# Who adds the state's part to the skip term: GpSimd instead of VectorE, in a state-space stage on one Trainium2 core

## The chip, the core and the metric

The kernel runs on one core of one Trainium2 chip. Its engines have queues of their own: TensorE (PE in the profile, its weight loads PEld), VectorE (DVE), ScalarE (ACT), GpSimd (POOL) and SyncE (SP, which here only starts transfers). They wait for each other through semaphores alone. The metric is device time in microseconds, median of the runs; lower is better.

## The reference, cut to what matters

The program is a stack of four layers on 1024 tokens of width 512 (2 sequences of 512): a state-space layer, a gated feed-forward layer, an attention layer and a mixture of experts, each followed by a layer norm and a residual. The change lies in the first. Its core, for each of 64 heads of 64 channels, is

```
state = state * dA_t[..., None, None] + dtx_t[..., None] * B_t[:, :, None, :]
y_t = jnp.einsum('bhpn,bhn->bhp', state, C_t)
...
y = jnp.moveaxis(ys, 0, 1) + x * D[None, None, :, None]
```

after which y is normalised over groups of 512 channels, multiplied by silu(gate), and projected back to width 512.

## The kernel before, in words

The state-space layer goes over 8 groups of 8 heads (512 channels). The first and the last group are written out, the six between are one hardware loop, so all engines repeat one pattern with a period of about 126 us. A group has 8 steps, s = 0 to 7, one for each block of 128 tokens; a sequence has 4 blocks, and c = (s - 1) % 4 is the place in its sequence of the block that is finished in step s. Work is pipelined over steps: step s prepares block s (transposes, decay masks), computes y of block s - 1, and projects the normalised yn of block s - 2. In steps 0, 1, 2, 4, 5 and 6 two convolution tiles of the next sequence or group go between (their taps on VectorE, their tanh on ScalarE); the last group has them only in steps 0 to 2.

For one block, y has three parts:

- the state's part, C times the carried state: TensorE writes it into bank 6 (L1352), VectorE scales it with the decays into `y` (L1060, signals `yo_used`); only where c > 0
- the part of the block's own 128 tokens, 16 matmuls on the diagonal block into bank 7 (L1358, signals `yi_ready`)
- the skip term `xd` = x * D, made by GpSimd one step earlier (L597, signals `xd_ready`)

VectorE adds the second (L1073, `y_part`) and then the third (L1076, `y_ready`). Where c = 0 there is no state's part, and one addition (L1080) does it. After `y`, in VectorE's order: the new state (L1089, which needs GpSimd's decayed state, L578), the first convolution tile's silu (L972), the taps of the second (L966, three), the gate (L1099), the second silu, the output's accumulation (L1106), and at the head of the next step `yn` (L1033), for which TensorE's transposes L1344 wait.

GpSimd's order in a step is: the two decay masks `am` of the next block (L551, these need `d_ready`, the end of TensorE's L1325), in step 2 the four low halves of the output weights (L299, `wol`), the state's decay (L578, c = 1 and 2), `dtx` (L588, needs the 16 matmuls done), `xdec` (L593), `xd` (L597, needs `y_ready`), and the two small operations of the normalisation (L602, L605). In step 3 two low halves of the next group's convolution weights follow (`wcl`, L299). TensorE's L1325 waits for the taps of all convolution tiles issued before it, since it writes a bank that they read.

The order of each engine is what is written in its `step` function; nothing schedules it anew.

Of the kernel before, what the change touches and what calls it, by code (L numbers as in the profile page):

```python
# [18 lines left out]
NT = NB * L // P  # L19
# [34 lines left out]
def program(nc, hidden, w_conv, w_gate, w_dt, conv_w, conv_b, dt_bias, A_log, Dskip, norm_w, w_out,  # L54
            ff_gu, ff_dn, gate_s, up_s, down_s, wq, wk, bqk, wv, bv, wo, bo, gate_w, expert_w, out):
    ctx = ExitStack()
    with ctx:
# [4 lines left out]
        def sem(name):  # L62
            return ctx.enter_context(nc.semaphore(name))
# [4 lines left out]
        def bk(i):  # L68
            return banks[:, i, :]
# [23 lines left out]
        def sa(name, shape, dt=F32):  # L93
            return sb(name, shape, dt, A)
# [26 lines left out]
        xd = sa("xd", [P, GI])  # L121
        bcast = xd[:, 0:2 * H].rearrange("p (a h) -> p a h", a=2)
        state = sa("state", [P, GI])
        y = sa("y", [P, GI])
# [111 lines left out]
        am_ready, xd_ready, xdec_ready, dtx_ready, sdec_ready = (sem(s) for s in ("am_ready", "xd_ready", "xdec_ready", "dtx_ready", "sdec_ready"))  # L236
        m_ready, yo_ready, yo_used, yi_ready, y_part, y_ready = (sem(s) for s in ("m_ready", "yo_ready", "yo_used", "yi_ready", "y_part", "y_ready"))
# [42 lines left out]
        def conv_stage(group):  # L280

            t = xbc[:, :, :].rearrange("p a b -> p (a b)") if group == 0 else x[:, :, :].rearrange("p a b -> p (a b)")
            return t[:, 0:KT * CT * P].rearrange("p (k c) -> p k c", k=KT)
# [3 lines left out]
        def pair(ap):  # L287
            return ap.rearrange("p (h c) -> p h c", h=HG)
# [8 lines left out]
        def low(eng, o, full, high):  # L297

            return eng.tensor_tensor(o, full, high.bitcast(F32), ALU.subtract)  # L299
# [23 lines left out]
        def entered(g, i):  # L323

            return (CH - 1) * NB * g + (CH - 1) * (i // CH)
# [42 lines left out]
        def heads(row):  # L368

            return cur[:, row, :].unsqueeze(2).to_broadcast([P, HG, HP])  # L370
# [162 lines left out]
        def _(pool):  # L533
# [14 lines left out]
            def decays(i):  # L548

                for part, a in enumerate((ah, al)):  # L550
                    m = pool.tensor_tensor(am[:, part, :, :], a[:, i, :].bitcast(F32).unsqueeze(2).to_broadcast([P, HG, P]),  # L551
                                           upto[:, :].unsqueeze(1).to_broadcast([P, HG, P]), ALU.mult)
                m.then_inc(am_ready, 1)
# [8 lines left out]
            def step(g, s, first, last):  # L562
                if s < NT and not (last and s == NT - 1):

                    pool.wait_ge(d_ready, NT * g + s + 1)
                    if s == NT - 1:
                        pool.wait_ge(ah_ready, g + 2)
                    decays((s + 1) % NT)
                if s == 2:
                    for k in range(KT):  # L570
                        pool.wait_ge(wo_hi, KT * g + k + 1)
                        low(pool, wol[:, k, :], out_stage[:, k, :], woh[:, k, :]).then_inc(wo_lo, 1)
                i = s - 1
                c = i % CH
                if s >= 1 and 1 <= c < CH - 1:

                    pool.wait_ge(yo_ready, entered(g, i) + c)
                    pool.tensor_tensor(pair(state[:, :]), pair(state[:, :]), heads(4 * NT + i),  # L578
                                       ALU.mult).then_inc(sdec_ready, 1)
                if s == 0:  # L580
                    pool.wait_ge(cur_ready, g + 1)
                if s < NT:

                    pool.wait_ge(x_out, NT * g + s + 1)
                    src = pair(xtok[:, s % 2, :])
                    if not (first and s == 0):
                        pool.wait_ge(yi_ready, NT * g + s)
                    pool.tensor_tensor(pair(dtx[:, :]), src, heads(NT + s), ALU.mult).then_inc(dtx_ready, 1)  # L588
                    if s % CH < CH - 1:
                        m = entered(g, s) + s % CH  # L590
                        if not (first and s == 0):
                            pool.wait_ge(st_ready, m)
                        pool.tensor_tensor(pair(xdec[:, :]), src, heads(3 * NT + s), ALU.mult).then_inc(xdec_ready, 1)  # L593
                if s < NT:
                    if not (first and s == 0):
                        pool.wait_ge(y_ready, NT * g + s)
                    pool.tensor_tensor(pair(xd[:, :]), src, heads(5 * NT), ALU.mult).then_inc(xd_ready, 1)  # L597
                if not (first and s == 0) and s <= NT:

                    n = NT * g + s  # L600
                    pool.wait_ge(ss_ready, n)
                    pool.tensor_tensor(ssv[:, i % 2:i % 2 + 1], ss[:, i % 2:i % 2 + 1], epsc[:, :],  # L602
                                       ALU.add).then_inc(ssv_ready, 1)
                    pool.wait_ge(ssv_ready, n)
                    pool.tensor_tensor(rg[:, i % 2:i % 2 + 1], ssv[:, i % 2:i % 2 + 1], mhalf[:, 0:1],  # L605
                                       ALU.pow).then_inc(rg_ready, 1)

                if s == 3 and not last:
                    for k in (2, 3):
                        pool.wait_ge(wc_hi, KT * g + KT + k + 1)  # L610
                        low(pool, wcl[:, k, :], conv_stage(1)[:, k, :], wch[:, k, :]).then_inc(wc_lo, 1)
                if s == NT - 1 and not last:
                    gate_low(g + 1)
                if last and s >= 3:
                    if s == 3:
                        pool.wait_ge(x_again, 16 * NT)
                    norm_pool(1, s - 3)

            def gate_low(g):
                for k in range(KT):  # L620
                    pool.wait_ge(wg_hi, KT * g + k + 1)
                    low(pool, wgl[:, k, :], gate_stage[:, k, :], wgh[:, k, :]).then_inc(wg_lo, 1)

            pool.wait_ge(ah_ready, 1)
            decays(0)
            gate_low(0)
            group_steps(pool, step)
            for n in range(NT - 1, ROUNDS):
                norm_pool(1, n)
            if STAGES >= 2:  # L630
                norm_wait(pool, 1, "tr", NT)
                pool.memset(acc[:, :, :], 0.0).then_inc(f_clear, 1)
                if STAGES >= 3:
                    c = Count(sel_ready)
# [22 lines left out]
                    for j, (base, step) in enumerate(((63, -1), (-64, 1))):  # L657
                        made(pool.affine_select(out=head[:, j:j + 1], in_=ones[:, 0:1], compare_op=ALU.is_ge, fill=0.0,
                                                base=base, pattern=[[0, 1]], channel_multiplier=step))
# [6 lines left out]
                for n in range(-2, ROUNDS):  # L666
                    if n >= 0:
                        norm_pool(2, n)
                    i = n + 2
# [278 lines left out]
        def _(dve):  # L948
# [70 lines left out]
            def step(g, s, first, last):  # L1019
# [7 lines left out]
                i = s - 2  # L1027
# [24 lines left out]
                i, c = s - 1, (s - 1) % CH  # L1052
                if not (first and s == 0) and s <= NT:
                    m = entered(g, i)
# [6 lines left out]
                i = s - 2  # L1061
# [5 lines left out]
                    low(nc.vector, ynTl[:, :], bk(4), ynTh[:, :]).then_inc(ynT_lo, 1)  # L1067
                i, c = s - 1, (s - 1) % CH
                if not (first and s == 0) and s <= NT:
                    if c > 0:  # L1070
                        dve.wait_ge(yi_ready, NT * g + i + 1)
                        dve.wait_ge(yo_used, m + c)
                        nc.vector.tensor_tensor(y[:, :], y[:, :], bk(7), ALU.add).then_inc(y_part, 1)  # L1073
                        dve.wait_ge(xd_ready, NT * g + i + 1)
                        dve.wait_ge(y_part, m + c)
                        nc.vector.tensor_tensor(y[:, :], y[:, :], xd[:, :], ALU.add).then_inc(y_ready, 1)  # L1076
                    else:
                        dve.wait_ge(yi_ready, NT * g + i + 1)
                        dve.wait_ge(xd_ready, NT * g + i + 1)
                        nc.vector.tensor_tensor(y[:, :], bk(7), xd[:, :], ALU.add).then_inc(y_ready, 1)  # L1080
                    if c < CH - 1:
                        dve.wait_ge(st_ready, m + c + 1)
                        if c == 0:
                            if not (first and s == 1):
                                dve.wait_ge(yo_ready, m)
                            nc.vector.tensor_copy(state[:, :], bk(6)).then_inc(state_ready, 1)
                        else:
                            dve.wait_ge(sdec_ready, (CH - 2) * NB * g + (CH - 2) * (i // CH) + c)
                            nc.vector.tensor_tensor(state[:, :], bk(6), state[:, :], ALU.add).then_inc(state_ready, 1)  # L1089
# [13 lines left out]
                i = s - 2  # L1103
                if not (first and s < 2):
                    dve.wait_ge(o_ready, NT * g + i + 1)
                    nc.vector.tensor_tensor(acc[:, i % NT, :], acc[:, i % NT, :], bk(1), ALU.add).then_inc(out_added, 1)  # L1106
                    if last and i >= 0:
                        norm_round(1, i)

            group_steps(dve, step)  # L1110
            norm_vector(1, NT)
            if STAGES >= 2:
# [45 lines left out]
            if STAGES >= 3:  # L1158
# [25 lines left out]
                for n in range(UNITS + O_BACK - 7):  # L1184
# [35 lines left out]
                    if piece:  # L1220
                        m, what, i, u = piece
# [444 lines left out]
```

## Time and profile before

| what | value |
|---|---|
| three runs | 1919.59 to 1921.9 us, median 1921.78 |
| the profiled execution | 1919.35 us, its span 1917.6 us |
| busy share of the span | PE 90%, DVE 69%, POOL 50%, ACT 38% |
| mean granted TensorE clock | 0.95 of full speed |
| the state-space groups in the span | about 88 to 1117 us |

The span runs from the first to the last instruction of the core; the execution's own time is 1.75 us longer. In the rows, a start and a duration are in us, the bracket at the end is the time that the engine stood idle before the instruction and who ended it, and an engine that is busy may still be blocked within an instruction: then its duration is longer than that of its fellows. One group serves as the pattern below: its step 2 is from 488.2 to 505.1 us.

### The profile page before, as it was taken

What the parts mean: (1) busy time and instruction counts of PE and PEld (TensorE: products, weight loads), DVE (VectorE), ACT (ScalarE), POOL (GpSimd) and SP (SyncE); (2) the same over time, 40 slices, a digit from 0 to 9 for tenths busy, and PEclk for the clock granted to TensorE, in tenths of its full rate; (3) what the DMA queues carried; (4) which work ended last, traced back from release to release, by engine and by line L of the source; (5) the groups of instructions that cost most, each with busy time, mean ns of one, the idle gap of its engine ahead of it and who ended that gap; (6) DMA issues with size and microseconds to landing.
All of it is one profiled execution on the core that took longest, in us unless ns stands there. A gap on an engine that the chain in (4) does not pass through costs nothing.

```text
span 1917.6 us, 25666 instructions
## 1 busy us (share of the span) xinstructions
PE 1725.5 (90%) x9030; PEld 1348.3 (70%) x9030; DVE 1316.7 (69%) x2025; ACT 728.0 (38%) x1338; POOL 966.5 (50%) x821
## 2 busy tenths in 40 slices
PE   3799999999999999999997769992899999878998
PEld 2578777777788777877786558881667776647886
DVE  4788787888777878788877555566267767663224
ACT  2443434434434344344352123330166766520010
POOL 3375676767757766677576441007333433151223
PEclk9899999999999999999998869995899999989999
DMA  3001020010100200101002002120000000101101
GB/s 128 1 34 45 1 77 1 33 44 0 53 24 0 77 0 33 44 0 77 0 1 77 1 28 75 68 77 33 0 12 1 12 1 1 46 4 63 44 22 44
DMA packets 16290, 61.31 MB, mean 32 GB/s; under 512 B 5472, under 2 KB 5600, under 8 KB 10976
## 3 DMA queue, kind: packets, MB, share of 16 engines
q1 hardware_dynamic: 16224, 60.44, 8.7%
q8 instruction: 40, 0.66, 0.1%
q14 instruction: 26, 0.21, 0.0%
HBM read 58.34 MB, written 2.10 MB: 32 GB/s over the span
## 4 chain that ended last, share of the span: by engine, by line
PE 70%; DVE 13%; POOL 8%; issue 5%; ACT 3%; SPq 0%; DMA 0%; POOLq 0%; DVEq 0%; ACTq 0%
PE banks L294 38%; PE banks L1426 6%; PE banks L1358 5%; PE banks L1545 3%; POOL wol L299 2%; PE banks L1436 2%; PE banks L1367 2%; PE banks L1504 2%; PE banks L1325 2%; PE banks L1352 2%; PE banks L1535 2%; DVE tap L966 2%; PE banks L1344 1%; DVE yn L1033 1%; DVE nmax L1189 1%
## 5 line engine op out<-in xcount | busy, mean ns | idle before, releaser
L966 DVE SCALAR_TENSOR_TENSOR tap<-banks,parg,tap 128x511 f32<-128x511 f32 (+2 forms) x288 | 214.8, 746 | 30.5 <-ACT tap L733 23.7
L551 POOL TENSOR_TENSOR am<-ah,upto 128x1024 fp32r<-128x1024 f32 x64 | 128.5, 2008 | 206.0 <-PE banks L1325 191.1
L688 POOL TENSOR_SCALAR kz<-kst,head 128x512 fp32r<-128x512 f32 x64 | 99.0, 1565 | 160.2 <-DVE kst L1173 160.2
L294 PE MATMUL banks<-xTh,wch 128*128 128x512 f32 x384 | 166.3, 433 | 3.1 <-POOL wcl L299 1.7
L1050 DVE TENSOR_TENSOR em<-em,gmask 128x1024 f32<-128x1024 f32 x64 | 130.9, 2046 | 49.1 <-ACT em L766 47.5
L551 POOL TENSOR_TENSOR am<-al,upto 128x1024 fp32r<-128x1024 f32 x64 | 160.3, 2505 | 0.0
L1358 PEld LDWEIGHTS banks<-dtx,em 128*128 128x128 f32 x1024 | 138.3, 211 | 28.8 <-issue 26.3
L294 PE MATMUL banks<-xTh,wcl 128*128 128x512 f32 x384 | 151.3, 394 | 0.0
L294 PE MATMUL banks<-xTl,wch 128*128 128x512 f32 x384 | 150.9, 393 | 0.0
L909 ACT ACTIVATE prob<-banks,nmax 128x128 f32<-128x128 f32 (+3 forms) x256 | 121.6, 529 | 55.1 <-DVE nmax L1189 54.9
L1358 PE MATMUL banks<-dtx,em 128*128 128x64 f32 x1024 | 134.9, 291 | 0.0
L1189 DVE TENSOR_REDUCE nmax<-banks 128x2 f32<-128x256 f32 (+3 forms) x128 | 104.7, 818 | 40.5 <-PE banks L1536 40.3
L1270 DVE SCALAR_TENSOR_TENSOR acc<-banks,we,acc 128x512 f32<-128x512 f32 x64 | 48.0, 751 | 121.1 <-PE banks L294 121.1
L733 ACT ACTIVATE tap<-banks,parg 128x512 f32<-128x512 f32 x96 | 74.6, 777 | 136.3 <-PE banks L294 128.7
L741 ACT ACTIVATE th<-tap 128x512 f32<-128x512 f32 x96 | 60.5, 631 | 152.4 <-DVE tap L966 149.6
L294 PE MATMUL banks<-wgh,xTh 128*128 128x512 f32 x256 | 111.9, 437 | 0.6 <-DVE tap L966 0.6
L294 PE MATMUL banks<-ewh,xTh 128*128 128x512 f32 x256 | 101.9, 398 | 5.2 <-DVEq L1266 5.2
L1545 PE MATMUL banks<-ident,prob 128*128 128x128 f32 x640 | 95.9, 277 | 10.6 <-DVE pB L1199 7.2
L294 PE MATMUL banks<-woh,ynTh 128*128 128x512 f32 x256 | 102.6, 401 | 1.5 <-DVE ynTl L299 1.5
L294 PE MATMUL banks<-wol,ynTh 128*128 128x512 f32 x256 | 102.4, 400 | 0.0
L294 PE MATMUL banks<-woh,ynTl 128*128 128x512 f32 x256 | 102.1, 399 | 0.0
L294 PE MATMUL banks<-wgl,xTh 128*128 128x512 f32 x256 | 101.3, 396 | 0.0
(244 smaller groups left out, 4622.2 us busy)
## 6 DMA issues: line engine op xcount, KB each, us to landing
x<-in_w_conv SPq DMA_DIRECT2D x7, 1536.0 KB, 6.6
x<-in_w_gate SPq DMA_DIRECT2D x8, 1024.0 KB, 4.8
x<-in_w_out SPq DMA_DIRECT2D x8, 1024.0 KB, 6.8
ew<-in_expert_w SPq DMA_DIRECT2D x8, 1024.0 KB, 4.8
gur<-in_ff_gu SPq DMA_DIRECT2D x7, 1024.0 KB, 4.9
x<-in_hidden SPq DMA_DIRECT2D x16, 256.0 KB, 4.0
dnr<-in_ff_dn SPq DMA_DIRECT2D x7, 512.0 KB, 3.4
out<-x SPq DMA_DIRECT2D x8, 256.0 KB, 2.0
```

The lines of the kernel that those rows point to most:

```text
L294: m = nc.tensor.matmul(o, a, b, start=first and n == 0, stop=last and n == len(terms) - 1)
L551: m = pool.tensor_tensor(am[:, part, :, :], a[:, i, :].bitcast(F32).unsqueeze(2).to_broadcast([P, HG, P]), upto[:, :].unsqueeze(1).to_broa ...
L688: m = pool.tensor_scalar(kz[:, quad % 2, p2, j, :], kst[:, p2, :].bitcast(F32), head[:, j:j + 1], None, ALU.mult)
L733: nc.scalar.activation(tap[:, q % 2, :], bk(CONV_BANKS[q % 2]), ACT.Identity, bias=parg[:, CT * KC + q:CT * KC + q + 1], scale=parg[:, KC ...
L741: nc.scalar.activation(th[:, :], tap[:, q % 2, :], ACT.Tanh).then_inc(tanh_ready, 1)
L909: e = nc.scalar.activation(prob[:, n % 2, j, 0:kw], bk(2 * (n % 2) + j)[:, 0:kw], ACT.Exp, bias=nmax[:, n % 2, j:j + 1])
L966: nc.vector.scalar_tensor_tensor(tap[:, q % 2, sh:L], bk(CONV_BANKS[q % 2])[:, 0:L - sh], parg[:, KC * q + k:KC * q + k + 1], tap[:, q % 2 ...
L1050: nc.vector.tensor_tensor(em[:, s % 2, :, :], em[:, s % 2, :, :], gmask[:, :].unsqueeze(1).to_broadcast([P, HG, P]), ALU.mult).then_inc(m_ ...
L1189: nc.vector.tensor_reduce(nmax[:, n % 2, :], banks[:, 2 * (n % 2):2 * (n % 2) + 2, 0:kw], AX, ALU.max, negate=True).then_inc(max_ready, 1)
L1358: m = mat(bk(7)[:, h * HP:(h + 1) * HP], em[:, i % 2, h, :], dtx[:, h * HP:(h + 1) * HP], start=True, stop=True)
L1426: m = mat(bk(2 * w + ft), gu[:, k, ft, w, :], part[:, k, tok], start=(k == 0 and part is xTh), stop=(k == KT - 1 and part is xTl))
L1545: m = pe.transpose(bk(4 + j)[:, c * P:(c + 1) * P], prob[:, w % 2, j, c * P:(c + 1) * P], ident[:, :])
```

## The change

GpSimd gets one more operation in each step with c > 0, right behind the state's decay: it adds the scaled state's part `y` onto the skip term, in place in `xd`. VectorE's two additions become one, `y` = bank 7 + `xd`, in the form that c = 0 had. `y_part` is now signalled by GpSimd. Nothing else moves; there are 48 such steps.

```diff
@@ GpSimd, step @@
                     pool.wait_ge(yo_ready, entered(g, i) + c)
                     pool.tensor_tensor(pair(state[:, :]), pair(state[:, :]), heads(4 * NT + i),
                                        ALU.mult).then_inc(sdec_ready, 1)
+                if (s >= 1 or not first) and s <= NT and c >= 1:
+
+                    pool.wait_ge(yo_used, entered(g, i) + c)
+                    pool.wait_ge(xd_ready, NT * g + s)
+                    pool.tensor_tensor(xd[:, :], xd[:, :], y[:, :], ALU.add).then_inc(y_part, 1)
                 if s == 0:
                     pool.wait_ge(cur_ready, g + 1)
@@ VectorE, step @@
                 i, c = s - 1, (s - 1) % CH
                 if not (first and s == 0) and s <= NT:
+                    dve.wait_ge(yi_ready, NT * g + i + 1)
                     if c > 0:
-                        dve.wait_ge(yi_ready, NT * g + i + 1)
-                        dve.wait_ge(yo_used, m + c)
-                        nc.vector.tensor_tensor(y[:, :], y[:, :], bk(7), ALU.add).then_inc(y_part, 1)
+                        dve.wait_ge(y_part, m + c)
+                    else:
                         dve.wait_ge(xd_ready, NT * g + i + 1)
-                        dve.wait_ge(y_part, m + c)
-                        nc.vector.tensor_tensor(y[:, :], y[:, :], xd[:, :], ALU.add).then_inc(y_ready, 1)
-                    else:
-                        dve.wait_ge(yi_ready, NT * g + i + 1)
-                        dve.wait_ge(xd_ready, NT * g + i + 1)
-                        nc.vector.tensor_tensor(y[:, :], bk(7), xd[:, :], ALU.add).then_inc(y_ready, 1)
+                    nc.vector.tensor_tensor(y[:, :], bk(7), xd[:, :], ALU.add).then_inc(y_ready, 1)
```

On GpSimd, in step 2 of a looped group, the queue before reads from the last of the four low halves on:

```order
L299 TENSOR_TENSOR wol<-x,woh 128x512 [waits wo_hi]
L578 TENSOR_TENSOR state<-state,cur 128x512 [waits yo_ready]
L588 TENSOR_TENSOR dtx<-xtok,cur 128x512 [waits yi_ready,x_out]
L592 REGISTER_ALU
L593 TENSOR_TENSOR xdec<-xtok,cur 128x512 [waits st_ready]
L597 TENSOR_TENSOR xd<-xtok,cur 128x512 [waits y_ready]
```

The same place on GpSimd in the changed kernel, whose lines below the insertion are numbered 5 higher:

```order
L299 TENSOR_TENSOR wol<-x,woh 128x512 [waits wo_hi]
L578 TENSOR_TENSOR state<-state,cur 128x512 [waits yo_ready]
L584 TENSOR_TENSOR xd<-xd,y 128x512 [waits xd_ready,yo_used]
L593 TENSOR_TENSOR dtx<-xtok,cur 128x512 [waits yi_ready,x_out]
L597 REGISTER_ALU
L598 TENSOR_TENSOR xdec<-xtok,cur 128x512 [waits st_ready]
```

The new addition L584 stands behind the low halves and the decay, and ahead of `dtx` and `xdec`.

On VectorE, in the same step 2, the stretch from the low half of `yn` to the second tile's first tap before is:

```order
L299 TENSOR_TENSOR ynTl<-banks,ynTh 128x512 [waits ynT_hi]
L1073 TENSOR_TENSOR y<-y,banks 128x512 [waits yo_used,yi_ready]
L1076 TENSOR_TENSOR y<-y,xd 128x512 [waits y_part,xd_ready]
L1082 REGISTER_ALU
L1088 ISA [waits st_ready]
L1089 TENSOR_TENSOR state<-banks,state 128x512 [waits sdec_ready]
L972 SCALAR_TENSOR_TENSOR xbc<-th,tap 128x512 [waits tanh_ready]
L961 REGISTER_ALU
L966 SCALAR_TENSOR_TENSOR tap<-banks,parg,tap 128x511 [waits tap0]
```

And the same stretch of VectorE in the changed kernel:

```order
L299 TENSOR_TENSOR ynTl<-banks,ynTh 128x512 [waits ynT_hi]
L1080 TENSOR_TENSOR y<-banks,xd 128x512 [waits y_part,yi_ready]
L1082 REGISTER_ALU
L1088 ISA [waits st_ready]
L1089 TENSOR_TENSOR state<-banks,state 128x512 [waits sdec_ready]
L977 SCALAR_TENSOR_TENSOR xbc<-th,tap 128x512 [waits tanh_ready]
L966 REGISTER_ALU
L971 SCALAR_TENSOR_TENSOR tap<-banks,parg,tap 128x511 [waits tap0]
```

One instruction is gone, and the one that is left waits for GpSimd's `y_part`.

## Rows read from the trace of the kernel before

**Rows 1.** The page, part 4: the chain that ended last, shares by engine
```profile
PE 70%; DVE 13%; POOL 8%; issue 5%; ACT 3%; SPq 0%; DMA 0%; POOLq 0%; DVEq 0%; ACTq 0%
```

**Rows 2.** Waits, 100 to 1110 us: total us, times, longest us
```profile
POOL dtx L588 <- PE banks L1358: 39.9, 36, 5.1
PE banks L1344 <- DVE yn L1033: 39.7, 13, 5.4
...
DVE state L1089 <- POOL state L578: 7.6, 8, 1.0
...
PE banks L1367 <- DVE y L1060: 3.9, 8, 0.5
...
PE banks L294 <- POOL wcl L299: 1.7, 4, 0.4
```

**Rows 3.** PE in order of time, steps 2 and 3: start, us, what
```profile
505.74 1.17 PE L1325 MATMUL banks<-am,after 128*128 128x512 f32 x4
509.49 0.66 PE L1344 MATMUL banks<-ident,yn 128*128 128x128 f32 x4 [2.58 <-DVE yn L1033]
```

**Rows 4.** DVE in order of time, steps 2 and 3
```profile
498.36 0.68 DVE L1073 TENSOR_TENSOR y<-y,banks 128x512 f32<-128x512 f32 x1
499.14 1.34 DVE L1076 TENSOR_TENSOR y<-y,xd 128x512 f32<-128x512 f32 x1
501.42 0.69 DVE L1089 TENSOR_TENSOR state<-banks,state 128x512 f32<-128x512 f32 x1 [0.94 <-POOL state L578]
502.03 0.91 DVE L972 SCALAR_TENSOR_TENSOR xbc<-th,tap 128x512 f32<-128x512 f32 x1
502.86 2.30 DVE L966 SCALAR_TENSOR_TENSOR tap<-banks,parg,tap 128x511 f32<-128x511 f32 x3
...
507.07 2.37 DVE L1033 SCALAR_TENSOR_TENSOR yn<-y,rg,sg 128x512 f32<-128x512 f32 x1
```

**Rows 5.** POOL in order of time, steps 2 and 3
```profile
493.89 6.04 POOL L299 TENSOR_TENSOR wol<-x,woh 128x512 fp32r<-128x512 f32 x4
499.90 1.49 POOL L578 TENSOR_TENSOR state<-state,cur 128x512 f32<-128x512 f32 x1
501.35 1.04 POOL L588 TENSOR_TENSOR dtx<-xtok,cur 128x512 f32<-128x512 f32 x1
502.35 1.49 POOL L593 TENSOR_TENSOR xdec<-xtok,cur 128x512 f32<-128x512 f32 x1
...
506.99 1.89 POOL L551 TENSOR_TENSOR am<-ah,upto 128x1024 fp32r<-128x1024 f32 x1 [1.37 <-PE banks L1325]
```

**Rows 6.** Instructions on `xd` by line: ns min/median/max
```profile
L1076 DVE TENSOR_TENSOR y<-y,xd x48: 691/1066/1408, 120.5 to 1106.0; 128x512 f32<-128x512 f32 x48
L1080 DVE TENSOR_TENSOR y<-banks,xd x16: 679/681/690, 104.1 to 1050.4; 128x512 f32<-128x512 f32 x16
```

**Rows 7.** POOL's L510 and L578, 100 to 1110 us: ns min/median/max
```profile
L510 POOL TENSOR_TENSOR x<-x,acc x5: 1262/1289/1302, 1039.2 to 1108.9; 128x512 f32<-128x512 f32 x5
...
L578 POOL TENSOR_TENSOR state<-state,cur x32: 1037/1041/1552, 121.2 to 1085.5; 128x512 f32<-128x512 f32 x32
```

**Rows 8.** PE by stretch: us, busy (instructions), granted clock, DMA, GB/s
```profile
384.00:387.30 3.30, 3.30 (x13) 0.51 0.00 0
...
510.30:516.90 6.60, 6.60 (x22) 0.50 0.00 0
```

**Rows 9.** POOL in step 7 of the same group
```profile
577.72 1.04 POOL L578 TENSOR_TENSOR state<-state,cur 128x512 f32<-128x512 f32 x1
```

**Rows 10.** DVE in step 7 of the same group
```profile
577.90 1.41 DVE L1076 TENSOR_TENSOR y<-y,xd 128x512 f32<-128x512 f32 x1
...
583.49 0.69 DVE L1106 TENSOR_TENSOR acc<-acc,banks 128x512 f32<-128x512 f32 x1 [1.42 <-PE banks L294]
```

**Rows 11.** The chain that ended last, in the last group's final step
```profile
1105.24 0.70 DVE y L1073
...
1106.03 0.70 DVE y L1076
```

## The prediction

> **What bounds the kernel now.** I read the page first, then the table of waits, then the engines in order of time. The chain of waits is TensorE's for 70% [rows 1]: a microsecond that VectorE saves counts only where TensorE waits for it. So the second view is who holds TensorE up. In the eight groups that is little and always at the same places [rows 2]: the transposes of yn (39.7 us in 13 waits), a bank that VectorE must free (3.9 us in 8), and GpSimd's low halves in step 3 (1.7 us in 4). One of these waits comes in each of the eight groups, 2.58 us long, in step 3 [rows 3]; the other five belong to the last group, which has no convolution to fill TensorE.
>
> The third view shows where the 2.58 us come from; the reader is to follow it from right to left. TensorE's L1344 starts at 509.49, when yn ends (507.07 + 2.37 = 509.44 [rows 4]). yn takes 2.37 us because GpSimd's first mask started at 506.99, 0.08 us ahead of it [rows 5]; it gets through 2.45 us after that start. Before yn comes a closed chain on VectorE: taps to 505.16 (502.86 + 2.30), silu to 502.94, the new state at 501.42. And that one waited 0.94 us for GpSimd's decay, which could not start before 499.90, because the four low halves hold GpSimd from 493.89 on. "DVE state waits for POOL state" stands 8 times in rows 2: in step 2 of every group VectorE is ahead of GpSimd, and GpSimd is what all wait for. There the change puts one more operation on GpSimd, ahead of what VectorE needs.
>
> **Prices.** Removed from VectorE, 48 times: L1073 at 0.68 us, and L1076 (0.69 to 1.41, median 1.07) turns into the form of L1080 (0.68 always) [rows 6]. Added on GpSimd, 48 times: an addition of two full 128x512 tiles. The trace has just that form, L510 at 1.29 us; the products with the small decays (L578 and its kin) take 1.04 [rows 7]. I take 1.29, the same operation and operands, and keep 1.04 and 1.49 (the blocked ones of rows 5) as the ends.
>
> The GPSIMD Engine Reference of the Trainium skill (section 3.1) gives 4497 ns for a two-input add of 2048 elements; a quarter of it is an estimate of 1.12 us. It lies between the two rows and would make the sum below about 1.4 us smaller. L510 has the measured duration, so 1.29 stays.
>
> **Step 2, worked out, all times in the pattern group [rows 3 to 5].**
> - The low halves end as before. The decay starts at 499.90; it was 1.49 us long because L1076 stood against it, and is now 1.04 (VectorE idles). The next start is 500.90 (starts of unblocked neighbours are 1.00 apart, as 501.35 and 502.35).
> - The addition ends at 500.90 + 1.29 = 502.19, and dtx starts at 502.15.
> - VectorE's single y starts 0.03 later, 502.22, as the state did behind the decay (501.39 to 501.42). The new state and the silu follow at 0.6 each (501.42 to 502.03 is 0.61): 503.43.
> - By then GpSimd is in xdec (503.15 to 504.19). The silu reads and writes SBUF alone, like the silu at 502.03, which took 0.91 and ended 0.56 after dtx did. So it ends at about 504.77 instead of 502.94: 1.83 us late, and the taps end at 506.99 instead of 505.16.
> - TensorE's L1325 stood at 505.74 and did not wait. Now it waits for the taps: 506.99 + 0.05 = 507.04, 1.30 us late.
> - The mask starts 1.25 behind that, 508.29. yn is issued at 507.07 + 1.83 = 508.90, again too late to be ahead, and ends 2.45 after the mask's start: 510.74. L1344 is 1.30 us late.
>
> That the loser waits for the whole instruction is what rows 4 and 5 show: L1076 lasts 1.34 and ends when the low half before the decay has ended plus its own 0.6; then the decay lasts 0.45 too long. The Trainium skill says the same (SBUF — State Buffer, "SBUF: two separate sides"): the pair of ports shared by VectorE and GpSimd is an exclusive lock, held for the instruction, by whoever starts first. With a shared bandwidth instead, the silu would end near 504.2 and TensorE be only some 0.75 us late, a sum of about 6 instead of 10.4 for this term.
>
> Everything behind L1344 is TensorE's own work up to the next step, so nothing gives the 1.30 us back. 8 groups x 1.30 = **+10.4 us**. Ends: with an addition of 1.04 and a silu that slips in ahead of xdec it is 0.45 each, +3.6; with 1.49 it is 1.5 each, +12.
>
> **The other steps.** In steps 3, 4 and 6 the addition falls into the hole in which GpSimd waits for the 16 matmuls before dtx (39.9 us in 36 waits [rows 2]) or delays dtx by at most 1 us, and dtx is needed a step later; VectorE arrives after it. In step 7 the decay runs from 577.72 to 578.76 [rows 9], so the addition ends at 580.0 and y at 580.7 instead of 579.31 (577.90 + 1.41) [rows 10]. Behind it VectorE has 1.42 us of idle time before L1106 alone; cost 0. In step 0 of the next group GpSimd is behind by one addition and VectorE by some 0.7 to 1 us; its idle time there swallows that too. If that cover were gone, one more us per group.
>
> **Gains.** In step 3 y is ready about 1 us earlier against TensorE, so GpSimd's wcl is no longer late: -1.7 us, the whole row of rows 2. In the last step of the last group both additions lie on the chain, 1105.24 to 1106.03 for the first [rows 11]: -0.8 us. Elsewhere the saved VectorE time lies in front of a wait.
>
> **The clock.** Some 3 us after the stall begins the granted clock falls to 0.50 (the 1.2 GHz level) for 3.3 us in one group and 6.6 us in the pattern group [rows 8]; each such us costs half. By the same view of all eight, five are of the short kind. After the change TensorE stands 1.30 us, works 0.95 on L1325, and stands 2.58 us again. If all five turned long that is 5 x 1.65 = +8.3; if none, 0. I take one or two: +2.5. This term is the least certain.
>
> **Sum:** 10.4 + 2.5 - 1.7 - 0.8 = +10.4 us on the profiled execution's 1919.35, 1929.8. The median of the runs is 2.4 us above that execution, so the forecast is **1932 us**.
>
> **Rivals.**
> - *yn gets ahead of the mask.* TensorE now waits for the taps, and the mask comes 1.30 after them; yn comes 1.91 after them. If L1325 ran at the lower clock (twice 1.17), the mask would come after 2.5 and yn would win: it would end at 509.6, L1344 start 0.15 late, and the groups cost nothing. 8 x 0.15 - 2.5 = -1.3: 1920.5. For it: the order turns on 0.6 us. Against: in rows 3 and 8 the clock fell only about 3 us into a stall, and L1325 would come after 1.3.
> - *The silu slips in.* xdec waits, or the addition is short, and only +3.6 is left: 3.6 - 2.5 = +1.1, 1923.
> - *Faster: the freed VectorE counts.* If the last group's five yn waits and its final step each gave back the 0.79 us of L1073, and wcl 1.7: -6.4, 1915. It decides where y_ready comes before TensorE's own next work ends. Against: in the last group's chain the addition appears once only; elsewhere TensorE's output products stand between y and yn.
> - *Worse: all five clocks go long, or step 0 has no cover:* +16 to +20, 1940.
>
> **How the numbers follow.** Forecast 0.70 (its own range 1925 to 1940); yn ahead 0.10; silu slips in 0.08; freed VectorE 0.06; worse 0.06. The range of eight in ten, 1920 to 1942, leaves out the faster case and the far ends. About 0.2% (3.8 us) is what a measurement of this kernel can tell from no change: below 1918 is faster, above 1925.6 slower. Faster 0.07, the same 0.16, slower 0.77.
>
> **What would show it.** In the profile after: in step 2 GpSimd's addition at about 1.29 us between decay and dtx; VectorE's y waiting for it, about 3 us of idle time in each group where 0.94 stood; L1325 waiting for "DVE tap" 8 times, about 1.3 us each; yn still long in step 3; no wait for wcl. If L1325 shows no wait, the forecast is wrong; if yn in step 3 takes 0.74, the first rival holds; if the groups' period stays near 126 us, the whole cost is.

## The result, and the profile after

| | before | changed |
|---|---|---|
| median of the runs | 1920.68 us (4 runs, 1918.36 to 1921.9) | 1944.68 us (4 runs, 1931.2 to 1948.33) |
| ratio | | 1.0114, 95% interval 1.0064 to 1.0163 |
| profiled execution | 1919.35 us, span 1917.6 | 1943.46 us, span 1941.7 |
| granted clock, mean | 0.950 | 0.942 |

The change makes the kernel slower, by 24 us in the medians and in the two profiled executions. The forecast was +10, 1932 us, and the range ended at 1942. The direction was right, and the place too, as the experiments show; the size was not.

The first view after is the table of waits, 100 to 1130 us, in the columns of [rows 2]:

```profile
DVE y L1080 <- POOL xd L584: 64.1, 24, 3.9
...
PE banks L1344 <- DVE yn L1038: 39.7, 13, 5.4
...
PE banks L1325 <- DVE tap L971: 13.5, 8, 2.2
...
PE banks L1367 <- DVE y L1065: 3.9, 8, 0.5
```

Against [rows 2], two of TensorE's waits are unchanged (39.7 and 3.9), the one for wcl has gone, and one is new: L1325 waits for the taps eight times, 13.5 us in all. VectorE's y waits for GpSimd's addition 24 times, where one wait for the decay stood in each group.

Step 2 of a looped group on GpSimd, answering to [rows 5]:

```profile
637.24 1.05 POOL L578 TENSOR_TENSOR state<-state,cur 128x512 f32<-128x512 f32 x1
638.24 1.29 POOL L584 TENSOR_TENSOR xd<-xd,y 128x512 f32<-128x512 f32 x1
...
640.48 1.05 POOL L598 TENSOR_TENSOR xdec<-xtok,cur 128x512 f32<-128x512 f32 x1
641.48 1.05 POOL L602 TENSOR_TENSOR xd<-xtok,cur 128x512 f32<-128x512 f32 x1
```

and on VectorE, answering to [rows 4]:

```profile
639.63 0.69 DVE L1080 TENSOR_TENSOR y<-banks,xd 128x512 f32<-128x512 f32 x1 [3.85 <-POOL xd L584]
640.24 0.68 DVE L1089 TENSOR_TENSOR state<-banks,state 128x512 f32<-128x512 f32 x1
640.84 2.27 DVE L977 SCALAR_TENSOR_TENSOR xbc<-th,tap 128x512 f32<-128x512 f32 x1
643.04 2.30 DVE L971 SCALAR_TENSOR_TENSOR tap<-banks,parg,tap 128x511 f32<-128x511 f32 x3
...
647.24 1.87 DVE L1038 SCALAR_TENSOR_TENSOR yn<-y,rg,sg 128x512 f32<-128x512 f32 x1
```

The chain is the forecast one up to the silu (L977): decay, addition of 1.29 us, y, state, silu issued 3.60 us after the decay's start (forecast 3.53). Then the silu lasts 2.27 us, where most of its kind take 0.69. It is blocked by xdec, which was running, and by xd behind it, which GpSimd started as soon as xdec ended; it finishes 0.58 us after xd. The forecast let it in after xdec.

TensorE in the same stretch, answering to [rows 3], and its granted clock by stretch (columns as in [rows 8]):

```profile
645.39 1.20 PE L1325 MATMUL banks<-am,after 128*128 128x512 f32 x4 [2.06 <-DVE tap L971]
649.17 1.11 PE L1344 MATMUL banks<-ident,yn 128*128 128x128 f32 x4 [2.58 <-DVE yn L1038]
```

```profile
646.60:649.10 2.50, 0.00 (x0) 0.59 0.00 0
649.10:657.10 8.00, 7.93 (x25) 0.50 0.00 0
```

TensorE stands idle 2.06 us, works 1.2, and stands idle 2.58. The clock falls to 1.2 GHz within the second pause and stays there for 8 us of work, where [rows 8] had 3.3 or 6.6. Seven of the eight groups have such a stretch of 10.2 us in all (1.0 to 2.3 of them in the pause), one has 3.4.

The new addition's durations, answering to [rows 6] (ns min/median/max):

```profile
L584 POOL TENSOR_TENSOR xd<-xd,y x48: 1262/1278/1297, 122.5 to 1126.7; 128x512 f32<-128x512 f32 x48
```

### The profile page after: what moved, and what is told of

It reads as the page before. It is cut to its first block, busy times and chain, and to the rows that moved or that the text cites. A ratio compares the mean times of both kernels' runs of the same rounds, so it can differ in the third digit from the quotient of the medians.

```text
span 1941.7 us, 25666 instructions
## 1 busy us (share of the span) xinstructions
PE 1737.9 (90%) x9030; PEld 1358.9 (70%) x9030; DVE 1270.9 (65%) x1977; ACT 725.9 (37%) x1338; POOL 1022.4 (53%) x869
## 4 chain that ended last, share of the span: by engine, by line
PE 75%; DVE 13%; POOL 5%; ACT 3%; issue 2%; SPq 1%; DMA 0%; POOLq 0%; DVEq 0%; ACTq 0%
PE banks L294 42%; PE banks L1358 6%; PE banks L1426 5%; PE banks L1545 3%; PE banks L1325 2%; PE banks L1436 2%; PE banks L1367 2%; PE banks L1352 2%; PE banks L1504 2%; PE banks L1535 2%; POOL wol L299 2%; PE banks L1344 2%; DVE tap L971 2%; PE banks L1311 1%; DVE nmax L1189 1%
## 5 line engine op out<-in xcount | busy, mean ns | idle before, releaser
L1358 PEld LDWEIGHTS banks<-dtx,em 128*128 128x128 f32 x1024 | 141.5, 216 | 29.0 <-issue 28.2
L1358 PE MATMUL banks<-dtx,em 128*128 128x64 f32 x1024 | 138.4, 295 | 0.0
```

Source lines behind the costliest of these rows:

```text
L1358: m = mat(bk(7)[:, h * HP:(h + 1) * HP], em[:, i % 2, h, :], dtx[:, h * HP:(h + 1) * HP], start=True, stop=True)
```

## The experiments

Each ratio is against the kernel before on the same chip. Its median was 1922.5 us beside the first four kernels below, 1919.7 beside the one with xd held and the three with only the low halves moved, and 1922.2 beside the changed kernel again and the three with both moves.

Several experiments are also read by one account. It covers the state-space layer, from the first L1325 to the last of the layer's output products, and adds up for the profiled execution TensorE's idle time and its work at 1.2 GHz, half of which is lost time. Before, these are 53.5 and 71.8 us; in the changed kernel 64.7 and 95.5. So 11.2 us of the loss are idle time and 11.8 (half of 23.7) are the clock, 23.0 together; the layer took 1060.1 us where it took 1036.2, and all that follows it 797.5 and 797.3.

### Where the loss arises: all steps but step 2

```diff
-                if (s >= 1 or not first) and s <= NT and c >= 1:
+                if (s >= 1 or not first) and s <= NT and c >= 1 and s != 2:
```

against the changed kernel, and with VectorE's two additions kept in step 2.

> The change in all steps but step 2, where GpSimd stands behind the four low halves; there the two VectorE additions stay. Theory (the whole loss is the wait behind the low halves in step 2 of each group, and what the clock makes of it): the loss is gone and the two gains are left, -1.7 us for the late wcl and -0.8 us at the end of the last group: 1918 us beside 1920.7, no wait of L1325 for a tap in step 3. Rival (40 more additions on GpSimd cost wherever they stand, by the shared port or by delaying its queue): five sixths of the 24 us stay, 1940 us.

Measured: 1917.61 us, ratio 0.9973 (0.9955 to 0.9990). Forty of the 48 additions cost nothing on balance; they gain a little. Its table of waits from 100 us on has no L1325 at all. But the wait for wcl, whose disappearance the theory had counted as a gain, is still there (3.2 us in 4 against 1.7 in 4 before). So the gain is real and its reason was not the one given. In its profile the stretches at 1.2 GHz behind step 3 of the eight groups are 10.2 us together (three of 3.4), where those of before are 37.5. By the account the work at 1.2 GHz fell from 71.8 to 49.3 us, worth 11.2, and what brought that about is open. TensorE's idle time rose from 53.5 to 60.3. 5.5 us of that are one wait in the first group, ahead of any addition: VectorE's mask product lasts 7.47 us, where it took 2.61 before, and ends only after five GpSimd instructions that follow each other without a pause (86.80 to 93.59; the first and the last are shown):

```profile
87.19 7.47 DVE L1055 TENSOR_TENSOR em<-em,gmask 128x1024 f32<-128x1024 f32 x1 [2.83 <-ACT em L771]
```

```profile
86.80 1.92 POOL L551 TENSOR_TENSOR am<-ah,upto 128x1024 fp32r<-128x1024 f32 x1
...
92.52 1.07 POOL L602 TENSOR_TENSOR xd<-xtok,cur 128x512 f32<-128x512 f32 x1
```

### Step 2 alone

The opposite condition: the new form only where s == 2, 8 additions.

> The change in step 2 alone, 8 additions on GpSimd instead of 48. Theory: nearly the whole loss, 1943 to 1948 us, with L1325 waiting 1.0 to 2.2 us for a tap in each of the eight groups. Rival (the loss is spread over all 48 additions): one sixth of it, 1925 us.

Measured: 1944.84 us, ratio 1.0117 (1.0096 to 1.0138), the whole loss from a sixth of the additions. TensorE's wait for the taps, 100 to 1160 us (L1325 is L1333 in this kernel):

```profile
PE banks L1333 <- DVE tap L971: 13.5, 8, 2.1
```

### GpSimd's time, or VectorE's wait

```diff
+                    if s == 2:
+                        pool.tensor_tensor(pair(dtx[:, :]), src, heads(NT + s), ALU.mult).then_inc(extra, 1)
+                        pool.wait_ge(extra, g + 1)
                     pool.tensor_tensor(pair(dtx[:, :]), src, heads(NT + s), ALU.mult).then_inc(dtx_ready, 1)
```

in the kernel before.

> The kernel before, in which GpSimd makes dtx twice in step 2 (the same product, 1.04 us, behind the decay, where the change puts its addition), but nothing waits for it in VectorE. Theory (what costs is that VectorE's y and all behind it wait for GpSimd, not GpSimd's microsecond): 1920 to 1923 us, no wait of L1325 for a tap. Rival (one more GpSimd operation there costs by holding the port against the silu or by making the masks late): L1325 waits about 0.6 us or more in each group, 1928 us or more.

Measured: 1919.56 us, ratio 0.9990 (0.9976 to 1.0004), no wait of L1325. A microsecond more on GpSimd at that place costs nothing that can be measured. What costs is that VectorE waits for it.

### How much of it is the clock

```diff
-                    for j in range(KT):
+                    for j in [j for _ in range(5 if s == 3 else 1) for j in range(KT)]:
                         m = pe.transpose(bk(4)[:, j * P:(j + 1) * P], xbc[:, j, tok], ident[:, :])
```

in the changed kernel.

> The changed kernel, in which TensorE makes the four transposes L1311 five times over in step 3 (the same result, 1.75 us more), in the time in which L1325 would stand idle. Theory (part of the loss is the lower clock that follows the longer idleness): L1325's wait shrinks to 0.3 us where it was 2.06, no later work moves by more than 0.7 us, and the stretch at 1.2 GHz behind it shrinks from 10.2 us per group to 6.8 or 3.4: 7 to 14 us faster than the change, 1931 to 1938 us. Rival (the idle time itself is the loss, the clock's part is small, as the prediction had it): 1945 us or up to 3 us above, since idle time is only replaced by idle work.

Measured: 1933.5 us, ratio 1.0061 (1.0038 to 1.0084): 11 us less than the change in the medians, from work that does nothing but fill a pause. TensorE in step 3 of one group (start, us, what), and its clock from 130 us to the same point of the last group, for this kernel, the changed one and the one before:

```profile
888.92 2.35 PE L1311 MATMUL banks<-ident,xbc 128*128 128x128 f32 x20
...
891.92 1.20 PE L1325 MATMUL banks<-am,after 128*128 128x512 f32 x4 [0.32 <-DVE tap L971]
895.70 0.66 PE L1344 MATMUL banks<-ident,yn 128*128 128x128 f32 x4 [2.58 <-DVE yn L1038]
```

```profile
130.00:1024.00 894.00, 866.81 (x4368) 0.99 0.08 31
```

```profile
130.00:1037.00 907.00, 871.00 (x4260) 0.96 0.08 30
```

```profile
130.00:1015.00 885.00, 860.15 (x4256) 0.98 0.08 31
```

L1344 still waits 2.58 us. L1325 waits 0.32 to 0.41 us in three groups, whose silus last 2.3 us like the one above; in the other five, whose silus last 1.24, it does not wait, and the 16 added transposes (1.75 us: 2.35 for 20, less 0.60 for 4) are longer than the pause. There L1325 starts 7.60 us after the decay's start instead of 7.12. Over the eight groups this distance adds up to 62.6 us, in the changed kernel's profile, which has five long silus and three short ones, to 62.3: the lateness of L1325 is still there in sum.

What has gone is the low clock: 0.99 instead of 0.96. It is even above the kernel before, whose profile had 0.98; the filler removes more than the change had added. By the account TensorE is idle 56.2 us and works 53.7 at 1.2 GHz. Against the changed kernel the clock gives 20.9 us back, and the filler costs some 6 (14.7 us more of work, worked out for the full clock, in the place of 8.5 of idle time). So the 11 us are what is left of a larger gain, and not themselves the clock's share in the change. That share is the 11.8 us of the account, nearly half of the 24.

### Why some waits of L1325 are 1.0 and others 2.1 us

```diff
                     if not (first and s == 0):
                         pool.wait_ge(y_ready, NT * g + s)
+                    if s == 2:
+                        pool.wait_ge(xbc_ready, NB * CT * g + conv_tiles(2, last)[0] + 1)
                     pool.tensor_tensor(pair(xd[:, :]), src, heads(5 * NT), ALU.mult).then_inc(xd_ready, 1)
```

> The changed kernel, in which GpSimd's xd of step 2 waits for the silu of the first tile, so that the silu is blocked by one GpSimd instruction (xdec) and not by two. Theory (the 2.06 us waits of L1325 are the 1.03 us ones plus one more GpSimd instruction of 1.03 us in front of the silu): all eight waits are about 1.0 us, 5 us less in all than the 13.5 us of the change, and a shorter stretch at 1.2 GHz where the clock's phase allows: 1930 to 1940 us. Rival (the two lengths have another cause): waits of 2 us stay, 1943 to 1947 us.

Measured: 1932.65 us, ratio 1.0064 (1.0050 to 1.0078), six runs within 1.5 us of each other. GpSimd, VectorE and the wait:

```profile
507.27 1.04 POOL L598 TENSOR_TENSOR xdec<-xtok,cur 128x512 f32<-128x512 f32 x1
508.94 1.04 POOL L604 TENSOR_TENSOR xd<-xtok,cur 128x512 f32<-128x512 f32 x1 [0.63 <-DVE xbc L979]
```

```profile
507.62 1.24 DVE L979 SCALAR_TENSOR_TENSOR xbc<-th,tap 128x512 f32<-128x512 f32 x1
```

```profile
PE banks L1327 <- DVE tap L973: 8.4, 8, 1.1
```

With one GpSimd instruction in front of it the silu takes 1.24 us, and all eight waits are 1.0 to 1.1 us. In the changed kernel three were of this length and five of the other. The 5.1 us of waits that went bring 12 us in the medians: the clock follows them again. In this profile its stretches behind the eight groups are 3.4 and 10.2 us in turn, and by the account the work at 1.2 GHz is 84.2 us instead of 95.5.

### The changed kernel again

Unaltered.

> The changed kernel once more, unaltered. Theory (its runs differ by how many of the eight silus of step 2 are blocked by one GpSimd instruction and how many by two, and by the clock's stretches behind that): runs from 1931, where all are blocked by one, as in the kernel with xd held, to 1948; L1325's waits of 1.0 and 2.1 us both appear, and the run's time rises with the number of the long ones. Rival (the 1931 us run was another disturbance): all runs between 1943 and 1948.

Measured: 1945.75 us, ratio 1.0126 (1.0101 to 1.0150), runs of 1935.14 to 1952.24. The execution at 1935.14 was the profiled one; its waits are

```profile
PE banks L1325 <- DVE tap L971: 9.4, 8, 2.1
```

one of 2.1 us and seven of 1.0 to 1.1, against 13.5 in the execution at 1943.46. One run lies above the 1948 us of the theory. The two profiles agree with the theory; the slower runs have none, so that they have five to eight long ones is argued, not shown.

### The low halves behind the addition

GpSimd's four `wol` of step 2 are moved from ahead of the decay to behind it:

```diff
-                if s == 2:
-                    for k in range(KT):
-                        pool.wait_ge(wo_hi, KT * g + k + 1)
-                        low(pool, wol[:, k, :], out_stage[:, k, :], woh[:, k, :]).then_inc(wo_lo, 1)
 ...
+                if s == 2:
+                    for k in range(KT):
+                        ...
                 if s == 0:
                     pool.wait_ge(cur_ready, g + 1)
```

once in the changed kernel (behind decay and addition), once in the one before, and once with the new additions in all steps but step 2.

> The changed kernel, in which GpSimd makes the four low halves of step 2 behind the decay and the new addition instead of ahead of them. Theory (the addition costs because it stands behind the low halves): VectorE's y no longer waits for GpSimd, L1325 for no tap; the state is ready 0.94 us earlier than in the kernel before, so yn can be issued ahead of the mask and its 2.58 us wait shrinks or goes. The low halves end about 1 us late for the output products and rg comes about 1 us later, which eats some: 1890 to 1910 us. Rival (the addition itself costs, by the port and by GpSimd's load, wherever it stands): at or above the 1922 us of before.

> The kernel before with the same move alone: the four low halves behind the decay, both additions on VectorE. Theory: the 0.94 us wait for the decay goes, yn is issued at about 506.1 in the pattern group's time instead of 507.07, ahead of the mask, and takes 0.74 instead of 2.37 us; the 2.58 us wait in step 3 of each group goes and with it the stretch at 1.2 GHz: 8 x (2.6 + 1.7) = 34 us, 1885 to 1895 us. Rival (another engine is just behind, so that TensorE waits as long for something else): 1915 to 1922 us.

> The low halves of step 2 behind the decay, and the change in all steps but step 2. Theory: the gain of the move alone and the one or two us of the 40 other additions: 1883 to 1893 us, at or a little below the move alone. Rival (what the additions gained elsewhere was the clock's phase and not their own work): as the move alone, or above it.

Measured: 1928.69 us, ratio 1.0036 (1.0022 to 1.0049), with the new additions everywhere; 1917.84 us, ratio 0.9988 (0.9970 to 1.0006), with the old; 1917.05 us, ratio 0.9986 (0.9973 to 0.9999), with the new in all steps but step 2, which is no different from the old. All three forecasts failed in the same way: the first half of the mechanism came true and the gain did not. In the second kernel:

```profile
503.21 0.74 DVE L1033 SCALAR_TENSOR_TENSOR yn<-y,rg,sg 128x512 f32<-128x512 f32 x1
...
507.76 1.22 DVE L1050 TENSOR_TENSOR em<-em,gmask 128x1024 f32<-128x1024 f32 x1 [3.40 <-ACT em L766]
```

```profile
505.24 1.57 ACT L763 CAST wch<-x 128x768 fp32r<-128x768 f32 x2 [1.85 <-DMA x<-in_w_conv]
506.71 1.02 ACT L766 ACTIVATE em<-banks 128x1024 f32<-128x1024 f32 x1
```

```profile
509.73 2.04 PE L1367 MATMUL banks<-xdec,btok 128*128 128x512 f32 x2 [2.47 <-DVE y L1060]
```

yn is ahead of the mask and takes 0.74 us, and L1344 does not wait in the seven groups that are not the last. But the exponential of the masks stands behind two weight casts on ScalarE that wait for a transfer, VectorE's mask product waits for it, y behind that, and L1367 for y: 2.47 us of idle time in the place of 2.58. This is the wait that lay hidden under the other.

With the new additions on top, L1344 and L1367 wait 27.4 and 28.2 us (25.7 and 25.2 with the old), and the output products wait 2.4 us in 8 for `wol`, which is now late. So even off the worst place the addition in step 2 costs 11.6 us in the medians (1928.69 against 1917.05).

### Both moves: the exponential ahead of the casts

```diff
-                if s == 3 and not last:
-
-                    act.wait_ge(wc_in, 16 * g + 32)
-                    for k in (0, 1):
-                        nc.scalar.copy(wch[:, k, :], conv_stage(1)[:, k, :]).then_inc(wc_hi, 1)
 ...
-                    for k in (2, 3):
+                    for k in range(KT):
```

on ScalarE, with the low halves moved as above: with the old additions, with the new ones in all steps but step 2, and with the new ones everywhere.

> The kernel before, with GpSimd's low halves behind the decay in step 2, and with ScalarE's exponential of the masks ahead of all four weight casts in step 3 instead of between them. Theory (with the low halves moved, yn is on time, and the 2.47 us that L1367 then waits for the scaled state's part come from ScalarE, whose casts wait for a transfer ahead of the exponential): both waits are gone in the seven groups that have such casts, and with them most of the 3.4 and 6.8 us stretches at 1.2 GHz: 7 x (2.5 + 1.7) = 29 us below the kernel before, 1886 to 1900 us. Rival (again another wait takes the place): 1912 to 1920 us.

> Both moves, and GpSimd's addition in all steps but step 2. Theory: the two moves' gain and 0 to 3 us more: 1884 to 1898 us. Rival (without the waits, TensorE sets the pace alone and the freed VectorE time is worth nothing): equal to the two moves alone.

> Both moves, and GpSimd's addition in every step. Theory (with the low halves behind it the addition still makes them, dtx, xdec, xd and rg 1.3 us later in step 2, and rg is then what yn waits for): 5 to 10 us above the two moves with the old additions, 1895 to 1908 us. Rival (the addition is free once it stands ahead of the low halves): equal to them.

Measured: 1909.98 us, ratio **0.9941** (0.9924 to 0.9959); 1919.01 us, 0.9974 (0.9959 to 0.9990); 1922.92 us, 0.9995 (0.9976 to 1.0014).

The first is the fastest kernel of this study, 12 us below the one before and 35 below the changed one. It misses its forecast of 1886 to 1900 by the next wait in line (waits from 100 to 1160 us):

```profile
PE banks L1339 <- DVE yn L1028: 25.7, 7, 5.4
PE banks L294 <- POOL wcl L299: 14.2, 7, 2.0
PE banks L1362 <- DVE y L1055: 8.2, 16, 0.6
```

The seven waits of 2.5 us for y (L1362 here) are down to 0.6, and in their place wcl is late: 2.0 us per group before the convolution tile of step 4. It is not the casts, now behind the exponential, that hold it up, but what stands ahead of it in GpSimd's own queue. In step 3 of one group the casts end at 507.12, and GpSimd takes up wcl only at 513.63, directly behind rg; in no group does GpSimd stand idle before wcl:

```profile
504.09 3.03 ACT L767 CAST wch<-x 128x768 fp32r<-128x768 f32 x4
```

```profile
512.51 1.15 POOL L605 TENSOR_TENSOR rg<-ssv,mhalf 128x1 f32<-128x1 f32 x1
513.63 3.62 POOL L299 TENSOR_TENSOR wcl<-x,wch 128x768 fp32r<-128x768 f32 x2
```

With that, TensorE's waits for yn, y and wcl are only 2.0 us shorter in all than before (48.1 against 50.1, 100 to 1160 us). The gain is the clock's: the stretches at 1.2 GHz behind step 3 of the first seven groups are 13.7 us together where they were 34.1, worth 10.2.

In the second kernel the wait for wcl is 18.3 us, 4.1 more: GpSimd's addition in step 3 stands ahead of wcl. The same stretches are 23.9 us, which costs another 5.1. Its median is 9 us higher, and its forecast, 1884 to 1898, is missed. Here even the forty harmless additions cost, and the theory that GpSimd's other additions are free held only while something else ended last.

The third misses its forecast too, and 13 us are lost in the medians against the first, more than the 5 to 10 expected. VectorE's yn does wait for rg (2.9 us in 7), but TensorE's wait for yn is only 1.7 us longer; that for wcl is 3.9 longer, 2.4 are new for `wol`, and that for y is 1.9 shorter. Together that is 6.1 us, about what lies between the two profiled executions (1916.81 and 1910.82); the rest of the 13 is not explained.

## Why the prediction was wrong

**What bounds the kernel, and where the addition hurts: right.** The wait of L1325 for the taps appeared in all eight groups, yn was blocked again, L1344's 39.7 us did not change, and wcl's wait went. The kernel with step 2 alone has the whole loss.

**The prices: right.** The addition took 1.28 us where 1.29 was taken, y 0.69.

**The step that failed first: the clock, "+2.5, one or two of five".** The prediction counted the groups in which 3.4 us at 1.2 GHz would turn into 6.6 and capped the stretch there. It became 10.2 in seven of eight. Adding up the profile by quarters of a microsecond, the eight stretches hold 75.1 us at 1.2 GHz, 13.5 of them while TensorE was idle, so 61.6 us of work at half speed: 30.8 us lost. Before it was 37.5 us, all under work: 18.8 lost. The term is +12.0; the account of the whole layer has +11.8. The filled pause shows from the other side that the low clock can be taken away and the lateness of L1325 kept.

**The second: the silu passes after xdec, "+1.30 us per group".** It did in three groups of eight (waits of 1.01 to 1.10 us, less than the 1.30 forecast) and in five GpSimd's next instruction went ahead of it (2.06 to 2.17). 13.5 us instead of 10.4. In the three, the chain came out as worked out: from the decay's start to L1325 it is 7.1 to 7.2 us (forecast 7.14, before 5.84), and the wait is shorter than 1.30 because TensorE's own work ahead of it now ends 6.1 us after the decay's start and not 5.84. In the five it is 8.15 to 8.25. The prediction had a rival in which the silu slips in ahead of xdec and none in which it is passed over twice.

**The gains.** -1.7 for wcl came. The -0.8 at the end of the last group did not. The two additions left the chain, as forecast, but its last step reads, in order of time,

```profile
1125.87 3.31 PE banks L1358 x16
1129.17 4.09 PE banks L294 x12
```

The output products, at the lower clock, end last now; from the end of L1358 to the start of yn it is 7.4 us, where it was 7.0.

**The sum with what was measured:** 13.5 + 12.0 - 1.7 = +23.8, against 24.1 between the two executions.

**The other steps at no cost: right on balance for this kernel**, as the kernel without step 2 shows, though that balance holds a gain of the clock that was not forecast; not for one whose wcl ends last.

**The rivals.** yn never got ahead of the mask. "Worse", at 0.06, was the right one in kind; its chance and its end, 1940 us, were too small because the clock's stretch was taken to be no longer than the longest seen before.

## What to carry to other kernels

Before an operation is moved to a less busy engine, look at what stands ahead of it in that engine's queue: half-idle GpSimd was the one all waited for in step 2. A pause added to a pause that TensorE already makes is to be priced with the clock: here each microsecond of new waiting cost nearly another one, more than the longest stretch in the old profile would allow. And when a wait is removed, look up what was to end just behind it: here three stood in a row, 2.6, 2.5 and 2.0 us deep.

## What the runs showed of the hardware that was not expected

- A VectorE instruction that works in SBUF alone and is blocked by GpSimd does not always come next when GpSimd's instruction ends. In one kernel, at the same place, it was let in after one instruction (1.24 us for a silu of 0.69) or after two (2.27 us), 3 and 5 times in one execution, 7 and 1 in another. In the kernel without step 2 a mask product was once blocked by five in a row (7.47 us, and 2.61 at the same place before), which no other profile here has, and TensorE lost 5.5 us. What decides between the two is open. Six runs of the changed kernel lie 17 us apart (1935.14 to 1952.24); with GpSimd held back at that place six lay within 1.5 us.
- The stretch at 1.2 GHz does not follow from the length of the pause alone. In four profiles (the changed kernel twice, step 2 alone, xd held), a wait of 2.05 to 2.17 us of L1325 ahead of the 2.58 us of L1344 was followed by 10.2 us in 11 cases of 11, a wait of 1.0 to 1.1 us by 10.2 in 13 of 21 and by 3.4 in the others.
- Work that computes nothing new made a kernel 11 us faster: 2.35 us of transposes (20 in the place of 4) in a pause of 1.0 to 2.2 us. The clock stayed at 2.4 GHz in four of eight groups, where it had fallen in all eight, and the stretch in the others was 3.4 or 6.8 us.
